# First table's ids by one broadcast transfer, its first rows through ScalarE's queue, a last gather group split in two

## The reference, cut to what matters

```python
e = jnp.stack([tbl_0[ids[:, 0]], ..., tbl_25[ids[:, 25]]], axis=1)      # 512 x 26 x 128
all_emb = jnp.concatenate([bottom[:, None, :], e], axis=1)              # 512 x 27 x 128
gram = jnp.einsum('bfd,bgd->bfg', all_emb, all_emb)
z = gram[:, triu_i, triu_j]                                             # 351 pairs
h = jnp.concatenate([z, bottom], axis=1)                                # 512 x 479
h = jnp.maximum(h @ W_top1 + b_top1, 0.0)                               # 479 -> 512
h = jnp.maximum(h @ W_top2 + b_top2, 0.0)                               # 512 -> 256
y = h @ W_top3                                                          # 256 -> 1
```

## Time and profile before

| | us |
|---|---|
| median of 3 runs | 100.95 (100.61 to 101.44) |
| profiled execution, its own time | 101.67 |
| its span in the trace | 99.9 |
| TensorE matmul busy | 94.6 (95%) |
| TensorE weight loads busy (beside the matmuls) | 82.0 (82%) |
| VectorE busy | 60.0 (60%) |
| ScalarE busy | 55.7 (56%) |
| GpSimd busy | 60.4 (60%) |

### The profile page before, as it was taken

How to read it: one execution, slowest core, us unless ns; L and a number is a source line. 1 busy time by engine, 2 the same in 40 slices (tenths; PEclk the granted TensorE clock), 3 DMA queues, 4 the chain that set the end, 5 groups by cost and what they waited for, 6 DMA issues and landing times.

```text
span 99.9 us, 3533 instructions
## 1 busy us (share of the span) xinstructions
PE 94.6 (95%) x1512; PEld 82.0 (82%) x1512; DVE 60.0 (60%) x152; ACT 55.7 (56%) x95; POOL 60.4 (60%) x63
## 2 busy tenths in 40 slices
PE   4999999999999999999999999999999698999992
PEld 4798778888888888888899888979899587998981
DVE  3499999999999997986793044007400091047010
ACT  3798578959899999984962022421424035212232
POOL 2678778777877778777787777777777700000000
PEclk9999999999999999999999999999999999999999
DMA  1897999559687564699722222222222210000000
GB/s 40 257 355 237 365 369 339 203 162 322 225 261 208 197 228 81 173 227 261 241 59 53 59 57 54 59 57 54 57 54 57 54 33 7 0 7 3 0 7 1
DMA packets 6414, 13.70 MB, mean 137 GB/s; under 512 B 1907, under 2 KB 2691, under 8 KB 6398
## 3 DMA queue, kind: packets, MB, share of 16 engines
q1 hardware_dynamic: 4406, 9.66, 28.5%
q0 software_dynamic: 1824, 3.74, 15.1%
q10 hardware_dynamic: 168, 0.07, 0.3%
HBM read 13.45 MB, written 0.01 MB: 135 GB/s over the span
## 4 chain that ended last, share of the span: by engine, by line
PE 89%; issue 4%; ACT 4%; DVE 1%; POOL 0%; ACTq 0%
PE acc L644 36%; PE acc L705 12%; PE acc L739 11%; PE ring L684 6%; PE acc L672 6%; PE ring L750 5%; PE acc L730 4%; PE acc L603 3%; PE acc L617 2%; PE ring L763 2%; PE ring L713 1%; ACT emb L425 1%; ACT onehot L399 1%; PE ring L774 1%; ACT far L378 1%
## 5 line engine op out<-in xcount | busy, mean ns | idle before, releaser
L347 POOL DMA_INDIRECT rows<-tbl,ids_sb x57 | 59.8, 1049 | 18.7 <-issue 17.1
L533 DVE TENSOR_SCALAR onehot<-far 128x512 fp32r<-128x512 f32 (+2 forms) x85 | 29.8, 407 | 1.7 <-ACT far L378 1.7
L644 PE MATMUL acc<-onehot,hi 128*128 128x512 f32 (+1 forms) x84 | 23.3, 401 | 0.0
L644 PE MATMUL acc<-onehot,lo 128*128 128x512 f32 (+1 forms) x84 | 22.0, 386 | 0.0
L555 DVE STREAM_TRANSPOSE pairs<-acc 128x832 f32<-128x832 f32 x4 | 4.2, 1050 | 25.3 <-PE acc L705 25.3
L644 PEld LDWEIGHTS acc<-onehot,lo 128*128 128x128 f32 x84 | 15.7, 188 | 3.2
L644 PEld LDWEIGHTS acc<-onehot,hi 128*128 128x128 f32 x84 | 15.1, 192 | 3.5 <-DVE onehot L533 0.8
L519 DVE TENSOR_TENSOR lo<-raw,hi 128x512 fp32r<-128x512 f32 (+1 forms) x24 | 16.8, 701 | 1.9 <-ACT hi L364 1.9
L364 ACT CAST hi<-raw 128x1024 fp32r<-128x1024 f32 (+1 forms) x11 | 12.0, 1091 | 6.1 <-issue 3.7
L463 ACT COPY emb<-ring 128x512 f32<-128x512 f32 (+2 forms) x16 | 8.9, 556 | 11.4 <-PE ring L684 11.2
L705 PE MATMUL acc<-emb 128*27 128x27 f32 x1024 | 12.8, 193 | 1.7 <-issue 0.9
(11 more groups left out here) (53 smaller groups left out, 74.2 us busy)
## 6 DMA issues: line engine op xcount, KB each, us to landing
raw<-looked SPq DMA_DIRECT2D x9, 512.0 KB, 4.7
raw<-looked SPq DMA_DIRECT2D x2, 640.0 KB, 5.4
ids_b<-ids SPq DMA_DIRECT2D x4, 256.0 KB, 5.5
rows<-tbl,ids_sb POOLq DMA_INDIRECT x57, 4.1
w1z<-w SPq DMA_DIRECT2D x3, 234.0 KB
raw<-looked SPq DMA_DIRECT2D x2, 256.0 KB, 3.4
w_sb<-w SPq DMA_DIRECT2D x1, 512.0 KB
bot<-bottom_t SPq DMA_DIRECT2D x1, 256.0 KB, 7.2
```

The costliest lines, as they stand in the source:

```text
L347: nc.gpsimd.indirect_dma_start(out=rows[:, t, slot, :], out_offset=None, in_=tables[table], in_offset=bass.IndirectOffsetOnAxis(ap=ids_sb[ ...
L533: ins = nc.vector.tensor_scalar(onehot[:, n % OH_RING, k, of], far[:, t % FAR_RING, of], float(KP * c), None, ALU.is_equal)
L644: mm = nc.tensor.matmul(acc[:, look_bank(t), 0:looked_up(t)], part_of[:, t % HL_RING, c * D:(c + 1) * D], onehot[:, n % OH_RING, k, 0:look ...
```

## The change

Table 0's ids come to all partitions by a transfer of their own (`ids_0`, 128 x 384 integers read from one row, SP's first transfer), and `difference(0)` reads that. The spreading matmul of table 0 and the two filler products behind the spreading are gone. The first half of table 0's rows is loaded by ScalarE's queue instead of SP's. ScalarE makes table 0's first one-hot ahead of the first `hi`, and the store of `idt_h` stands behind that `hi`; VectorE makes `idt_h` behind its first three one-hots instead of ahead of them. ScalarE makes the first one-hot of the last table right after that table's `far`, that is ahead of the steps `look` 9 and `part`. And tile 3's last group is cut in two: its two gathered tables stay a turn, (3, 3), and the block of table 0 becomes a turn of its own, (3, 4), with its own semaphore and ScalarE copy.

```diff
--- before.py
+++ after.py
@@ -62,7 +62,6 @@
 LOOK = 4
 
 WARM_UP = 3
-WARM_ON = 2
 OH_RING = 4
 
 PARTS = 2
@@ -80,10 +79,14 @@
 SECOND = (4, 6, 8)
 
 
+def turns_of(t):
+
+    return TURNS + (t >= FIRST_TILES)
+
+
 def group(t, g):
 
-    slots = GROUPS[g]
-    return range(slots[0], NG + 1) if g == TURNS - 1 and t >= FIRST_TILES else slots
+    return range(NG, NG + 1) if g == TURNS else GROUPS[g]
 
 
 def looked_up(j):
@@ -119,7 +122,7 @@
               ("l1", 0, 1), ("gram", 1, (12, 32)), ("bottom", 1, 1), ("l1", 0, 2), ("l1", 0, 3), ("turn", 2, 3),
               ("l2", 0, 0), ("pairs", 1, 0), ("gram", 2, (0, 12)), ("turn", 3, 0), ("l1", 1, 0), ("bottom", 2, 0),
               ("gram", 2, (12, 16)), ("turn", 3, 1), ("l1", 1, 1), ("l1", 1, 2), ("gram", 2, (16, 32)), ("l1", 1, 3),
-              ("l2", 1, 0), ("turn", 3, 2), ("bottom", 2, 1), ("turn", 3, 3), ("pairs", 2, 0), ("gram", 3, (0, 20)),
+              ("l2", 1, 0), ("turn", 3, 2), ("bottom", 2, 1), ("turn", 3, 3), ("turn", 3, 4), ("pairs", 2, 0), ("gram", 3, (0, 20)),
               ("l1", 2, 0), ("l1", 2, 1), ("l1", 2, 2), ("gram", 3, (20, 32)), ("l1", 2, 3), ("l2", 2, 0),
               ("pairs", 3, 0), ("bottom", 3, 0), ("bottom", 3, 1), ("l1", 3, 0), ("l1", 3, 1), ("l1", 3, 2),
               ("l1", 3, 3), ("l2", 3, 0), ("l2", 3, 1), ("columns", 0, 0), ("l3", 3, 0)]
@@ -208,6 +211,7 @@
         lo = sb("lo", [KP, HL_RING, MAX_KC * D], F32R)
         onehot = sb("onehot", [KP, OH_RING, MAX_HALF, B], F32R)
         row_i = sb("row_i", [KP, 1], I32)
+        ids_0 = sb("ids_0", [128, FIRST_TILES * LANES], I32)
         scrap = sb("scrap", [KP, 1])
         neg_row = sb("neg_row", [KP, 1])
         neg_second = sb("neg_second", [KP, 1])
@@ -231,7 +235,7 @@
         w1b_in = sem("w1b_in")
         first_raw_in = sem("first_raw_in")
         raw_in = [sem(f"raw_in{k}") for k in range(RAW_RING)]
-        rows_in = [[sem(f"rows_in{t}_{g}") for g in range(TURNS)] for t in range(TILES)]
+        rows_in = [[sem(f"rows_in{t}_{g}") for g in range(turns_of(t))] for t in range(TILES)]
         out_done = sem("out_done")
         ident_set = sem("ident_set")
         ones_set = sem("ones_set")
@@ -242,6 +246,7 @@
         lo_ready = sem("lo_ready")
         idb_in = [sem(f"idb_in{k}") for k in range((NL - FIRST) // 2)]
         idt_in = sem("idt_in")
+        id0_in = sem("id0_in")
         idt_zero = sem("idt_zero")
         idt_ready = sem("idt_ready")
         idt_stored = sem("idt_stored")
@@ -291,8 +296,8 @@
                              ids_16[FIRST + 2 * k:FIRST + 2 * k + 2, :].rearrange("j b -> (j b)").unsqueeze(0)
                              .broadcast_to([128, 2 * B])).then_inc(idb_in[k], 16)
 
+            sp.dma_start(ids_0[:], ids_t[0:1, 0:looked_up(0)].broadcast_to([128, looked_up(0)])).then_inc(id0_in, 16)
             sp.dma_start(idt_i[:], ids_t).then_inc(idt_in, 16)
-            load_rows(0, 0, chunks(0) // 2, first_raw_in)
             load_rows(0, chunks(0) // 2, chunks(0), raw_in[0])
             load_rows(1, 0, chunks(1), raw_in[1])
             sp.wait_ge(first_raw_in, 16)
@@ -340,7 +345,7 @@
                                     pattern=[[-1, 128]], channel_multiplier=1).then_inc(ident_set, 1)
             pool.wait_ge(ids_in, 16)
             for t in range(TILES):
-                for g in range(TURNS):
+                for g in range(turns_of(t)):
                     for slot in group(t, g):
                         table = (GATHERED + LOOKED_UP)[slot]
                         col = t * TABLES + table
@@ -365,8 +370,11 @@
                                ).then_inc(hi_ready, 2)
 
             def difference(j):
-                if j < FIRST:
-                    act.wait_ge(ids_spread, j + 1)
+                if j == 0:
+                    act.wait_ge(id0_in, 16)
+                    of = ids_0[:]
+                elif j < FIRST:
+                    act.wait_ge(ids_spread, j)
                     of = acc[0:KP, spread_bank(j), 0:looked_up(j)]
                 else:
                     act.wait_ge(idb_in[(j - FIRST) // 2], 16)
@@ -378,7 +386,17 @@
                 nc.scalar.activation(far[:, j % FAR_RING, 0:looked_up(j)], of, ACT.Abs,
                                      bias=neg_row[:]).then_inc(far_ready, 1)
 
+            def first_chunk(j):
+                n = 2 * j
+                act.wait_ge(far_ready, j + 1)
+                if n >= OH_RING:
+                    act.wait_ge(oh_used, n - OH_RING + 1)
+                nc.scalar.activation(onehot[:, n % OH_RING, 0, 0:looked_up(j)], far[:, j % FAR_RING, 0:looked_up(j)],
+                                     ACT.Relu, bias=1.0, scale=-1.0).then_inc(oh_act, 1)
+
             act.dma_start(ids_sb[:], ids).then_inc(ids_in, 16)
+            half = chunks(0) // 2 * D
+            act.dma_start(raw[:, 0, 0:half], looked[0][:, 0:half]).then_inc(first_raw_in, 16)
 
             act.wait_ge(row_ready, 1)
             act.wait_ge(second_set, 1)
@@ -389,16 +407,13 @@
                     if t == 0:
 
                         difference(0)
+                    n = 2 * t
+                    if t < NL - 1:
+                        first_chunk(t)
+                    if t == 0:
+                        split(0, 0)
                         act.wait_ge(idt_ready, 1)
                         act.dma_start(ids_16, idt_h[:]).then_inc(idt_stored, 16)
-                        split(0, 0)
-                    n = 2 * t
-                    act.wait_ge(far_ready, t + 1)
-                    if n >= OH_RING:
-                        act.wait_ge(oh_used, n - OH_RING + 1)
-                    nc.scalar.activation(onehot[:, n % OH_RING, 0, 0:looked_up(t)], far[:, t % FAR_RING, 0:looked_up(t)],
-                                         ACT.Relu, bias=1.0, scale=-1.0).then_inc(oh_act, 1)
-                    if t == 0:
                         split(0, 1)
                         difference(1)
                     if 0 < t < HL_RING:
@@ -415,6 +430,8 @@
                                              bias=1.0, scale=-1.0).then_inc(oh_act, 1)
                     if 0 < t < NL - 1:
                         difference(t + 1)
+                    if t == NL - 2:
+                        first_chunk(NL - 1)
                 elif step == "look":
                     if t + HL_RING < NL:
                         split(t + HL_RING)
@@ -508,7 +525,6 @@
             dve.wait_ge(idt_in, 16)
             dve.wait_ge(idt_zero, 1)
             nc.vector.tensor_copy(idt[0:NL, :], idt_i[:]).then_inc(first_ready, 1)
-            nc.vector.tensor_copy(idt_h[:], idt_i[:]).then_inc(idt_ready, 1)
 
             def rest(t, half):
 
@@ -535,6 +551,9 @@
                             if n == 0 and k < chunks(t) // 2 - 1:
                                 ins.then_inc(oh_first, 1)
                         ins.then_inc(oh_dve, 1)
+                        if n == 0:
+
+                            nc.vector.tensor_copy(idt_h[:], idt_i[:]).then_inc(idt_ready, 1)
                         rest(t, half)
                     if t == NL - 1:
 
@@ -613,10 +632,9 @@
 
                     pe.wait_ge(pick_ready, 1)
                     pe.wait_ge(first_ready, 1)
-                    for n in range(FIRST):
+                    for n in range(1, FIRST):
                         nc.tensor.matmul(acc[:, spread_bank(n), 0:looked_up(n)], pick[:, n:n + 1].broadcast_to([128, 128]),
                                          idt[:, 0:looked_up(n)], start=True, stop=True).then_inc(ids_spread, 1)
-                    warm(WARM_ON)
                 elif step == "look":
                     if t >= LOOK:
 
@@ -694,7 +712,7 @@
                             pe.wait_ge(pairs_ready, 2 * t)
 
                         pe.wait_ge(emb_part, t + 2 if t < TILES // PARTS else 4)
-                        pe.wait_ge(emb_turned, turn_count(t, TURNS - 1))
+                        pe.wait_ge(emb_turned, turn_count(t, turns_of(t) - 1))
                     for k in range(start, end):
                         unit, at = divmod(k, UNIT)
                         if t == 0 and k == UNIT:
```

## The result

The changed kernel takes 105.84 us (median of 4 runs, 104.54 to 106.55) against 100.84 (4 runs): 1.0426 times the kernel before, 95% interval 1.0369 to 1.0482. Ratios here leave out executions over 1.5% above the fastest of their kernel (106.55 in this case), so they are not quotients of the medians. So the change is slower by 4 to 5%, where 100.75 us and no difference were forecast, and outside the range of 99.9 to 102.0. The profiled execution is the fastest of the four (104.54, span 102.8 against 99.9), so its trace shows 2.9 us of the loss.

The account below looks back on a forecast made before the run. TensorE's matmuls were taken as busy 95% of the span, with VectorE bounding the head. Head 0, last one-hot -0.3 and split +0.1 gave -0.2 us, so 100.95 became 100.75 us, range 99.9 to 102.0.

Parts of the forecast that it names:

- Start of table 0: Kernel's head: ids_0 lands 2.7 us after issue, at 3.5; VectorE starts at about 4.16, 0.35 us sooner.
- rival A: First transfer: the one-row broadcast is slow; at 5.5 us the kernel takes 103.55 us, halfway 102.15; chance 0.12.
- What moves VectorE's start moves TensorE at 19.2: Head: VectorE runs without a gap, so a shift of its start shifts TensorE at 19.2 us by as much.
- TensorE's part: Ahead of table 0: less spreading and fillers, TensorE there at about 5.2 instead of 5.58; worth 0, VectorE sets the pace.
- rival B: Table 0: TensorE stays slow for longer with fewer fillers, 1.75 us, giving 102.5, half of it 101.6; chance 0.08.
- The cast that moves: Head: the idt_h cast, now among VectorE's one-hots, costs about 0.41 us on the path; head so far about 0.
- Last table's first one-hot: Last table: made early in ScalarE's idle time, it removes TensorE's wait of 0.29 us; gain 0.3 us.
- The split group: Tile 3's last group: makes nothing ready sooner, pairs waits for another copy; cost 0.1 us, between 0 and 0.45.
- ScalarE's order: Head: hi of table 1 comes 0.6 us later, at 8.9, just in time for VectorE; taken as 0.
- signs of being wrong: Profile of the head: far of table 0 after 4.3, 0.33 us loads beyond 7 us, or VectorE waiting for table 1's hi.

Follow-up runs that it names:

- own_rows: Changed kernel with ids_0 read from 128 source rows of its own instead of one row: 102.71 to 104.41 us, against 101.12 for the kernel before.
- own_rows_raw_sp: Changed kernel with ids_0 from 128 source rows and the first half of table 0's rows back on SP's queue: 1.0141 times the kernel before.
- extra_own_rows: Kernel before, plus an unread 192 KB transfer from 128 source rows put first in SP's queue: 1.0183 times the kernel before.
- extra_broadcast: Kernel before, plus an unread one-row broadcast of table 0's ids put first in SP's queue: 1.0263 times the kernel before.
- raw_on_sp: Changed kernel with the first half of table 0's rows back on SP's queue, behind the ids: 1.0290 times the kernel before.
- mended: Changed kernel with ids_0 from 128 source rows, first rows on SP's queue, cast and store early, tile 3's group whole: 1.0109 times the kernel before.
- more_fillers: Changed kernel with 9 filler products ahead of the spreading instead of 3: 1.0596 times the kernel before.
- fillers_throughout: Changed kernel with 14 filler products ahead of the spreading instead of 3, and 3 behind it: 1.1086 times the kernel before.

## Why the prediction was wrong

**The step that failed: "Start of table 0".** It priced `ids_0` at 2.7 us by its size between two rows, and took 5.5 us of `ids_b` as a bound that wouldn't apply. From own rows it was 2.7 to 2.9. From one row it was 4.8, and VectorE started at 6.25 where 4.16 was forecast. That was rival A, "All 128 partitions read one row", at a chance of 0.12. The row for it stood there, 5.5 us for a broadcast against 3.0 for the same bytes from own rows, and was argued away as queueing. But even rival A at its upper price gives 103.55 us, and 105.84 were measured: the slow broadcast alone is not the answer, and the next two paragraphs matter as much.

**What the step left out.** It priced the new transfer and not its neighbours. SP's `idt_i` stands behind `ids_0`, and VectorE must take it in (L510, now L527) ahead of its first one-hot: the working forgot this wait. In the changed kernel both are ready together (the cast of `idt_i` ends at 6.23, `far` at 6.21), so `far` alone made sooner would have given nothing at VectorE's start; in own_rows `far` is ready at 4.18, and VectorE's one-hots stand at 4.49, behind the cast of `idt_i` at 4.15. It also left out the first rows. "What moves VectorE's start moves TensorE at 19.2" fails when `hi` is late: in own_rows_raw_sp VectorE started as forecast and then waited 1.31 us. Bytes put first delay what stands behind them: 1.8% with nobody reading them (extra_own_rows).

**"TensorE's part ... worth 0"** was wrong for the same reason as rival B's chance of 0.08 was too low: TensorE did become the slower engine, 4.52 us for table 0 against 2.99 when kept at work. As the sole cause the missing fillers are refuted (extra_broadcast has them all and loses 2.6%). That the slow stage lengthened is shown; what it cost the kernel is not, as the two runs that removed or moved it were slower. (Rival B's 0.49 us is the mean of one product of 384 and three of 512 columns; the changed kernel's three of 512 take 0.54 each. It changes little.)

**"The cast that moves"** and the last one-hot. The cast was sized at 0.41 us on VectorE's path; the path was TensorE's by then. What it cost was another thing, a gather issue of 3.6 to 4.3 us: between nothing and 1% of the time in the changed kernel, where TensorE was late anyway, but about 1 us in raw_on_sp and 1.1 at own_rows' first turn. GpSimd wasn't looked at in that step.

**Last table's first one-hot**: the wait went as said (0.36 us), the gain of 0.3 didn't arrive: 0.9996. **The split group**: no gather was late in the kernel before, and it costs, as said; 0.1 us was too small, 0.37 measured, inside the bounds of 0 to 0.45. The working let `pairs` start behind a short copy (0.3 us); with the waits for two copies, 0.25 and 0.33 us, it starts 0.97 us behind turn (3, 3).

**ScalarE's order** was put at 0. It can't be judged by itself, but in mended, with an early `far`, its first `hi` is 1.20 us later than before. All three signs of being wrong came true: `far` at 5.60 (named: later than 4.3), loads of 0.29 to 0.35 us until 11.2 (0.33 beyond 7), and VectorE's wait of 0.19 us for `hi` of table 1.

**What the 4.3% are made of** the runs show in part. Undone one after the other, the ratio goes from 4.3% to 2.9 (first rows back on SP's queue), to 1.4 (own source rows), to 1.1 (cast and store early, group whole; this last step is inside the intervals). The 1.5% between raw_on_sp and own_rows_raw_sp aren't the price of the single source row, since the long gather issue went in the same step; with nothing else changed the row cost 0.8% and the bytes 1.8. The prices come from different bases, and depend on what else is late.

## What to carry to other kernels

When a transfer is put first, price what stands behind it, in its own queue and in the others, and every in-order engine that must take one of these in before it can go on. Count its bytes against what the first rows need in the same stretch; and a broadcast from a single row isn't priced by its bytes. When an operation moves on one engine, look at the others too: here a 0.4 us cast moved on VectorE made GpSimd's gathers late, and the wait for them came 10 to 70 us later. Of an engine that stands still longer, ask at what pace it starts again.

## What the runs showed of the hardware

- 192 KB to 128 partitions as the first transfer: 2.7 to 2.9 us from 128 source rows, 4.1 to 5.2 from one row of 1.5 KB. The 52 KB beside it, on the other queue: 2.5 to 3.1 and 3.2 to 5.4 us; alone 2.0.
- One gather issue of 3.6 to 4.3 us instead of 0.9 to 1.9, which ended 0.6 us behind VectorE's first gap, in six kernels, and only with a 12 x 512 cast by VectorE a little ahead of it.
- TensorE was fast behind 9 fillers (0.18 us a load, granted clock 1.00, the level of 2.4 GHz) and slow again (0.32, granted clock 0.51, the level of 1.2 GHz) after standing still for 1.44 and 0.73 us with three products between (more_fillers). In the first slow stage of the changed kernel the loads are as slow and the column reads 1.00.
- Fourteen filler products more at the start went with gaps of up to 2.07 us without a releaser 70 to 85 us later (fillers_throughout). The cause stays open.
